# Squares for the norm bounds moved from VectorE to GpSimd in an attention and mixture-of-experts kernel

## The chip, the cores and the metric

The kernel runs on 8 cores of one Trainium2 chip. Each core takes one of the 8 batch entries (4096 tokens of width 1024) and runs the same program; the cores exchange nothing. The metric is the device time in microseconds (us) of the slowest core; lower is better.

## What is computed

The reference, cut to its core (16 heads of 64, 16 experts of inner width 512 of which the two best count, one shared expert of width 1024):

```python
def attn(x, Wq, Wk, Wv, Wo, bo):
    q, k, v = (x @ Wq), (x @ Wk), (x @ Wv)            # split into 16 heads
    w = softmax(q @ k.T / sqrt(64))
    return (w @ v) @ Wo + bo
def ffn(x, Wr, Wg, Wu, Wd, Sg, Su, Sd):
    shared = silu(x @ Sg) * (x @ Su) @ Sd
    cw = top-2 of softmax(x @ Wr), as a weight per token and expert
    routed = sum over e of (silu(x @ Wg[e]) * (x @ Wu[e]) @ Wd[e]) * cw[e]
    return routed + shared
x = layernorm(x + attn(x))
x = layernorm(x + ffn(x))
```

## The kernel before

The program is written as five instruction lists, one per engine, each run in order (`Prog.emit`; waits on semaphores are worked out from the `deps`). DMAs may be issued by SyncE, ScalarE and GpSimd. All DMAs of GpSimd that load weights or x count on one semaphore, and each waits for the one before it to have landed.

Stages: attention for the first 2048 queries (`attention_half(0)`), output projection and first layer norm for them (`wo_ln1_half(0)`), the same two for the other 2048 queries (`attention_half(1)`, `wo_ln1_half(1)`), and then the experts (`ffn_all`, from about 3480 us on).

An attention half runs over 8 pairs of heads `p` (128 channels), and in each over 4 query tiles `q` of 512. A tile has 32 steps `j` of 128 keys: two score matmuls (L528, L536), one exponential over 1024 columns on ScalarE (L551) and two matmuls with the values (L563, L571). The scores of step j+2 are issued in step j. The exponential has a bias that bounds the scores: minus the root of (largest squared norm of a query of the tile) times (largest squared norm of a key of the pair). These norms are what the change is about:

- Keys, `k_group` and `knorm_one`. `k_group(s, ki, kst)` makes 512 keys: 8 matmuls (L246), a VectorE copy from PSUM to `kt_v` (L253), a VectorE multiplication of these keys with themselves into `sqk[ki % 2]` (L260). `v_group` then makes 512 values with 32 short matmuls (L310) and two VectorE copies (L318, L325). `knorm_one` sums the squares over the channels with one TensorE matmul against ones (L272), VectorE takes the largest (L278) and merges it (L290). In the first half the keys and values of pair p+1 are made during the last query tile of pair p, one group ki after each fourth step (j = 3, 7, ... 31), and after pair 7 those of pair 0 once more for the second half. So there are 8 such windows with 8 groups each. Pair 0 of the first half gets its own from `kv_full` at the start. In the second half keys and values are read back instead (`kv_load_slice`: SyncE loads 8 slices of each, L344 and L350, after the same steps; each waits for the one before it to land).
- Queries, `q_chain_A` and `q_chain_B`. A: 8 matmuls (L412), a scaled VectorE copy into `qtb` (L420). B: a VectorE multiplication into `sqk[q % 2]` (L432), a TensorE sum (L444) and a VectorE maximum (L450). In the second half the chains of query tiles 0, 1, 2 of pair p+1 run in the last tile of pair p (A after steps 5, 9, 13, B one step later); that of tile 3 runs at the start of pair p+1. For pair 0 of the second half all four A and then all four B run at its start, and in the first half this holds for every pair.
- `q_chain_C_all` makes the bias from the four maxima (L464 to L487); the first exponential of a pair waits for it. `tail` divides the sums of the tile before by a VectorE reciprocal (L669, 6.5 us) and two multiplications (L674, L681); it is issued after step 2 of a tile.

What GpSimd's list holds during attention: only DMA issues. `load_qkv(p+1)` (L202) is emitted at the start of pair p and waits until the buffer's last user, `q_chain_A` of pair p-1, is done. After `attention_half(0)` comes the load of the output weights `wb[1][:, 0:8192]` (L1289), which has no `deps` beyond the weight DMA before it; the matmuls L720 of `wo_ln1_half(0)` read it. GpSimd's first multiplications (L1175) come in the expert stage.

## Time and profile before

| | |
|---|---|
| two timed runs | 6785.51 and 6828.65 us, median 6807.08 |
| the profiled execution | 6785.92 us |
| its span, slowest core (core 7) | 6784.4 us; the others from 6758.3 |
| mean granted TensorE clock of the cores | 0.942 to 0.945 |
| TensorE matmuls busy | 6045.8 us (89%) |
| VectorE busy | 2475.7 us (36%) |
| ScalarE busy | 2608.7 us (38%) |
| GpSimd busy | 729.6 us (11%), nearly all of it in the expert stage |

Busy times are sums over one profiled execution. Times in the trace are counted from the span's start. A row of the timeline gives the start, the duration, the engine (PE is TensorE, DVE VectorE, ACT ScalarE, POOL GpSimd; SPq is the queue of SyncE), the line and operation, and in brackets the idle time of that engine before it and what ended it.

### The profile page before, as it was taken

How to read it: one execution, taken by the hardware profiler on the slowest of the kernel's cores; microseconds unless marked ns; L12 is line 12 of the kernel's file. 1: busy time of each engine (PE TensorE's matmuls, PEld its weight loads, DVE VectorE, ACT ScalarE, POOL GpSimd, SP SyncE). 2: the span in 40 equal slices, each digit the busy share in tenths (PEclk: the TensorE clock that was granted, in tenths of full speed). 3: DMA queues.
4: the chain of work that ended last, by engine and by line, in shares of the span. 5: the costliest groups of instructions: out<-in, count | busy, mean ns of one | idle time of the engine just before them, and what ended most of it. 6: DMA issues, size and time to landing. Idle time of an engine off the chain costs nothing.

```text
span 6784.4 us, 78807 instructions; the slowest of 8 cores (6758.3 to 6784.4 us)
## 1 busy us (share of the span) xinstructions
PE 6045.8 (89%) x27000; PEld 2209.2 (33%) x27000; DVE 2475.7 (36%) x3406; ACT 2608.7 (38%) x2903; POOL 729.6 (11%) x683
## 2 busy tenths in 40 slices
PE   5898888888878888888889999999989999999995
PEld 2332233322322222222234444444433444444442
DVE  2333333333532222222433344434432443444345
ACT  2576655676257777777421111111122111111111
POOL 0000000000000000000001222222232222222220
PEclk8899989999889999989899999999999999999998
DMA  4000000000000000000112222222212222221111
GB/s 77 18 1 18 18 18 18 21 10 18 1 30 18 18 18 18 18 13 13 19 45 37 38 38 38 38 38 38 38 44 62 38 38 38 38 38 32 34 29 50
DMA packets 54615, 198.44 MB, mean 29 GB/s; under 512 B 5072, under 2 KB 27728, under 8 KB 37984
## 3 DMA queue, kind: packets, MB, share of 16 engines
q0 software_dynamic: 26496, 136.36, 11.3%
q1 hardware_dynamic: 25280, 44.46, 1.9%
q10 hardware_dynamic: 2464, 12.58, 0.5%
q8 instruction: 240, 3.93, 0.2%
q14 instruction: 135, 1.11, 0.1%
HBM read 291.85 MB, written 37.88 MB: 49 GB/s over the span
## 4 chain that ended last, share of the span: by engine, by line
PE 66%; ACT 17%; DVE 7%; issue 6%; DMA 4%; DVEq 0%; ACTq 0%; SPq 0%; POOLq 0%
ACT pt L551 16%; PE psA L1203 15%; PE psS L1150 15%; PE psS L1137 11%; PE psS L528 4%; PE psA L563 4%; PE psV L1137 4%; PE psA L571 3%; PE psS L720 2%; PE psV L310 2%; PE psM L246 1%; DVE recipb L669 1%; DMA wbB<-scr 1%; PE psM L658 1%; DMA xt<-xti 1%
## 5 line engine op out<-in xcount | busy, mean ns | idle before, releaser
L551 ACT ACTIVATE pt<-psS,biasb 128x1024 bf16<-128x1024 f32 x2048 | 2104.5, 1158 | 660.0 <-PE psS L536 622.4
L1158 ACT ACTIVATE sq<-psS 128x512 bf16<-128x512 f32 x432 | 257.9, 597 | 2251.1 <-PE psS L1137 2245.2
L528 PE MATMUL psS<-qtb,wbB 64*128 64x512 bf16 x2048 | 813.3, 402 | 199.0 <-ACT pt L551 86.4
L1164 DVE TENSOR_TENSOR abuf<-psS,sq 128x512 bf16<-128x512 f32 x576 | 398.4, 692 | 1615.8 <-PE psS L1150 1606.6
L563 PE MATMUL psA<-pt,wbA 128*65 128x512 bf16 x2048 | 874.3, 427 | 30.2 <-ACT pt L551 25.5
L536 PE MATMUL psS<-qtb,wbB 64*128 64x512 bf16 x2048 | 832.9, 412 | 0.0
L571 PE MATMUL psA<-pt,wbA 128*65 128x512 bf16 x2048 | 826.9, 404 | 0.0
L1175 POOL TENSOR_TENSOR abuf<-abuf,qtb 128x512 bf16<-128x512 bf16 x512 | 585.5, 1151 | 1558.4 <-DVE abuf L1164 1557.9
L1203 PE MATMUL psA<-abuf,wbB 128*128 128x512 bf16 x2304 | 560.4, 383 | 56.2 <-DVE xt L1231 21.4
L1203 PE MATMUL psA<-abuf,wbA 128*128 128x512 bf16 x2304 | 546.2, 379 | 21.7 <-ACT abuf L1223 4.7
L528 PEld LDWEIGHTS psS<-qtb,wbB 64*128 64x128 bf16 x2048 | 187.3, 94 | 1156.3 <-issue 1156.3
L1231 DVE TENSOR_TENSOR xt<-psA,xt 128x512 bf16<-128x512 f32 x544 | 376.3, 692 | 156.8 <-PE psA L1203 135.0
L1231 DVE TENSOR_TENSOR abuf<-psA,abuf 128x512 bf16<-128x512 f32 x544 | 376.3, 692 | 154.0 <-PE psA L1203 135.0
L626 DVE COPY astg<-psA 65x512 f32<-65x512 f32 x64 | 43.7, 682 | 1041.6 <-PE psA L571 1041.6
L669 DVE RECIPROCAL recipb<-recipb 64x1024 f32<-64x1024 f32 x64 | 418.9, 6545 | 6.6
L563 PEld LDWEIGHTS psA<-pt,wbA 128*65 128x65 bf16 x2048 | 225.7, 110 | 566.0 <-issue 566.0
L1203 PEld LDWEIGHTS psA<-abuf,wbB 128*128 128x128 bf16 x2304 | 197.2, 97 | 398.3 <-issue 230.8
L1203 PEld LDWEIGHTS psA<-abuf,wbA 128*128 128x128 bf16 x2304 | 195.1, 96 | 361.1 <-issue 190.7
L202 POOL DMA_DIRECT2D wbA<-attnw x14 | 7.4, 530 | 2677.1 <-PE psV L412 2677.1
L1150 PE MATMUL psS<-xt,wbB 128*128 128x512 bf16 x1152 | 273.5, 380 | 2.5 <-DVE abuf L1164 2.5
L1150 PE MATMUL psS<-xt,wbA 128*128 128x512 bf16 x1152 | 273.8, 381 | 0.0
L1150 PE MATMUL psS<-abuf,wbA 128*128 128x512 bf16 x1152 | 273.3, 380 | 0.0
(168 smaller groups left out, 5387.9 us busy)
## 6 DMA issues: line engine op xcount, KB each, us to landing
wbA<-moew POOLq DMA_DIRECT2D x54, 1024.0 KB, 7.9
wbB<-moew POOLq DMA_DIRECT2D x54, 1024.0 KB, 7.8
wbA<-attnw POOLq DMA_DIRECT2D x16, 768.0 KB, 7.0
scr<-wbA SPq DMA_DIRECT2D x8, 1040.0 KB, 4.1
xt<-xti POOLq DMA_DIRECT2D x8, 1024.0 KB, 8.9
scr<-wbB SPq DMA_DIRECT2D x8, 1024.0 KB, 3.9
out<-astg SPq DMA_DIRECT2D x16, 512.0 KB, 2.8
wbA<-scr SPq DMA_DIRECT2D x56, 130.0 KB, 2.1
```

The costliest lines, as they stand in the source:

```text
L528: e.matmul(psS[sl][:, 0:QT], kt_v[0:64, j * 128:(j + 1) * 128], qtb[0:64, sl_q * QT:(sl_q + 1) * QT], start=True, stop=True),
L536: e.matmul(psS[sl][:, QT:E2], kt_v[64:128, j * 128:(j + 1) * 128], qtb[64:128, sl_q * QT:(sl_q + 1) * QT], start=True, stop=True),
L551: e.activation(pt[:, sl * E2:(sl + 1) * E2], psS[j % 2][:, 0:E2], AF.Exp, bias=biasb[:, sl_q:sl_q + 1]),
L563: e.matmul(psA[0][0:65, :], va_v[:, j * 130:j * 130 + 65], pt[:, sl * E2:sl * E2 + QT], start=(j == 0), stop=(j == NJ - 1)),
L571: e.matmul(psA[1][0:65, :], va_v[:, j * 130 + 65:j * 130 + 130], pt[:, sl * E2 + QT:sl * E2 + E2], start=(j == 0), stop=(j == NJ - 1)),
L669: lambda e: e.reciprocal(recipb[:, 0:E2], recipb[:, 0:E2]),
L1137: e.matmul(gp[:, go:go + QT], wb[sl][:, kc * 512 + fc * 128: kc * 512 + (fc + 1) * 128], xsrcs[h](kc, q), start=(kc == 0), stop=(kc == NCH ...
L1150: e.matmul(up[:, uo:uo + QT], wb[sl][:, 4096 + kc * 512 + fc * 128: 4096 + kc * 512 + (fc + 1) * 128], xsrcs[h](kc, q), start=(kc == 0), s ...
L1164: e.tensor_tensor(abuf[:, hb + fc * QT:hb + (fc + 1) * QT], up[:, uo:uo + QT], sq[:, :], ALU.mult),
L1175: e.tensor_tensor(abuf[:, hb + fc * QT:hb + (fc + 1) * QT], abuf[:, hb + fc * QT:hb + (fc + 1) * QT], qtb[:, q * QT:(q + 1) * QT], ALU.mult),
L1203: e.matmul(pa[:, 0:QT], wb[sl][:, 8192 + fc * 1024 + mc * 128: 8192 + fc * 1024 + (mc + 1) * 128], abuf[:, hb + fc * QT:hb + (fc + 1) * QT ...
L1231: e.tensor_tensor(acc_ap(h, mc, q), pa[:, 0:QT], acc_ap(h, mc, q), ALU.add),
```

## The change

The multiplications of `k_group` in the windows of the first half (8 pairs times 8 groups, 64 in all) and those of `q_chain_B` in the second half (8 pairs times 4, 32 in all) go from VectorE to GpSimd. They signal GpSimd's semaphore instead of VectorE's. Those of `kv_full` and of `q_chain_B` in the first half stay on VectorE. The instructions stand in GpSimd's list where the calls emit them, between the DMA issues.

```diff
-            def k_group(s, ki, kst):
+            def k_group(s, ki, kst, eng2="vector"):
...
-                sqt = P.emit("vector",
+                sqt = P.emit(eng2,
                              lambda e, ki=ki:
                                  e.tensor_tensor(sqk[:, (ki % 2) * QT:(ki % 2 + 1) * QT],
                                                  kt_v[:, ki * QT:(ki + 1) * QT],
                                                  kt_v[:, ki * QT:(ki + 1) * QT],
                                                  ALU.mult),
-                             deps=[ev, war["sqk%d" % (ki % 2)]], inc="dve",
+                             deps=[ev, war["sqk%d" % (ki % 2)]],
+                             inc="pl" if eng2 == "gpsimd" else "dve",
                              nochain=True)
...
                 def q_chain_B(q, qe):
...
-                    qs = P.emit("vector",
+                    qs = P.emit("gpsimd" if h == 1 else "vector",
...
-                                deps=[qe, war["sqk%d" % (q % 2)]], inc="dve",
+                                deps=[qe, war["sqk%d" % (q % 2)]],
+                                inc="pl" if h == 1 else "dve",
                                 nochain=True)
...
                             if h == 0:
-                                k_group(ns[1], ki, nkst)
+                                k_group(ns[1], ki, nkst, eng2="gpsimd")
```

## Rows read from the trace of the kernel before

**Rows 1.** The page: shares of the chain that ended last, by engine.

```profile
PE 66%; ACT 17%; DVE 7%; issue 6%; DMA 4%; DVEq 0%; ACTq 0%; SPq 0%; POOLq 0%
```

**Rows 2.** Waits of TensorE: total us, times, longest; the first from L444's own view.

```profile
  DVE sqk L432: 92.1, 64
...
PE psM L272 <- DVE sqk L260: 34.4, 8, 5.6
PE psS L528 <- DMA wbB<-scr: 32.1, 7, 6.6
```

**Rows 3.** View of line 1175, a GpSimd multiplication: ns min/median/max, first and last start.

```profile
L1175 POOL TENSOR_TENSOR abuf<-abuf,qtb x512: 1138/1152/1169, 3628.1 to 6688.0; 128x512 bf16<-128x512 bf16 x171
```

**Rows 4.** Timeline, second group (ki = 1) of pair 0's window, first half.

```profile
259.27 0.69 DVE L253 CAST wbB<-psM 128x512 bf16<-128x512 f32 x1 [5.59 <-PE psM L246]
260.06 0.42 DVE L260 TENSOR_TENSOR sqk<-wbB 128x512 bf16<-128x512 bf16 x1
260.81 0.38 PE L272 MATMUL psM<-sqk,ones_c 128*1 128x512 bf16 x1
...
261.61 3.12 ACT L551 ACTIVATE pt<-psS,biasb 128x1024 bf16<-128x1024 f32 x3 [3.58 <-PE psS L536]
```

**Rows 5.** Timeline, first group (ki = 0) of the same window.

```profile
250.69 0.69 DVE L253 CAST wbB<-psM 128x512 bf16<-128x512 f32 x1
...
252.06 0.38 PE L272 MATMUL psM<-sqk,ones_c 128*1 128x512 bf16 x1 [3.94 <-DVE sqk L260]
```

**Rows 6.** Timeline, after the last group (ki = 7) of the same window.

```profile
307.27 1.89 PE L412 MATMUL psM<-xt,wbA 128*128 128x512 bf16 x8 [1.73 <-DVE rowsA L290]
```

**Rows 7.** Timeline in the expert stage: VectorE to GpSimd and back.

```profile
5020.50 0.69 DVE L863 CAST ab<-psM 128x512 bf16<-128x512 f32 x1 [0.17 <-DVE xt L1231]
5021.33 2.12 POOL L1052 TENSOR_TENSOR outst<-xt,ab 128x1024 f32<-128x1024 bf16 x1 [21.86 <-DVE ab L863]
...
5023.51 0.69 DVE L1118 CAST qtb<-psM 128x512 bf16<-128x512 f32 x1 [1.00 <-POOL outst L1052]
```

**Rows 8.** Output weights: GpSimd's issue, the last copy of keys, first reading matmuls.

```profile
1352.55 0.53 POOL L1289 DMA_DIRECT2D wbB<-woi  x1 [6.66 <-DMA wbA<-attnw]
...
1744.26 0.69 DVE L253 CAST wbB<-psM 128x512 bf16<-128x512 f32 x1 [3.45 <-PE psM L246]
...
1753.38 3.60 PE L720 MATMUL psS<-abuf,wbB 128*128 128x512 bf16 x8
```

**Rows 9.** DMA issues: KB each, us from issue to landing.

```profile
wbB<-woi POOLq DMA_DIRECT2D x1, 2048.0 KB, 14.9
```

**Rows 10.** Timeline, second half, pair 1's window, chain B of query tile 2.

```profile
2250.00 0.38 PE L444 MATMUL psM<-sqk,ones_c 128*1 128x512 bf16 x1 [0.60 <-DVE sqk L432]
```

**Rows 11.** Timeline, second half, start of pair 2, then of pair 6.

```profile
2268.65 0.69 DVE L420 TENSOR_SCALAR qtb<-psV 128x512 bf16<-128x512 f32 x1 [17.49 <-PE psV L412]
2269.15 0.53 POOL L202 DMA_DIRECT2D wbA<-attnw  x1 [173.35 <-PE psV L412]
...
2277.99 3.19 ACT L551 ACTIVATE pt<-psS,biasb 128x1024 bf16<-128x1024 f32 x3 [4.76 <-DVE biasb L487]
...
2968.02 0.69 DVE L420 TENSOR_SCALAR qtb<-psV 128x512 bf16<-128x512 f32 x1 [17.70 <-PE psV L412]
...
2973.65 3.19 ACT L551 ACTIVATE pt<-psS,biasb 128x1024 bf16<-128x1024 f32 x3 [1.05 <-DVE biasb L487]
```

**Rows 12.** Timeline of SyncE's queue, pair 1's window: keys 3, keys 7, values 7.

```profile
2251.39 0.32 SPq L344 DMA_DIRECT2D wbB<-scr  x1
...
2270.22 0.32 SPq L344 DMA_DIRECT2D wbB<-scr  x1
...
2276.35 0.32 SPq L350 DMA_DIRECT2D wbA<-scr  x1
```

**Rows 13.** Timeline, start of the second half: last chain A, last sum of B.

```profile
1916.18 0.69 DVE L420 TENSOR_SCALAR qtb<-psV 128x512 bf16<-128x512 f32 x1 [2.25 <-PE psV L412]
...
1922.68 0.58 PE L444 MATMUL psV<-sqk,ones_c 128*1 128x512 bf16 x1 [1.26 <-DVE sqk L432]
```

## The prediction, made before the changed kernel ran

> **What bounds the kernel now.** I read the page first. Its chain of work that ended last lies two thirds on TensorE and hardly on VectorE [rows 1], so freeing VectorE is worth little by itself. The question is what stands behind each square: a TensorE matmul that sums it, and TensorE runs its list in order. The waits say where that already hurts: the sums of the queries' squares (L444) waited 64 times, the sums of the keys' squares (L272) 8 times, and the scores (L528) 7 times for a slice of keys [rows 2]. Then the timeline around one case of each kind, and GpSimd's and SyncE's queues.
>
> In a window of the first half the second group shows the usual case. The copy of the keys starts at 259.27, VectorE squares them at 260.06 for 0.42 us, done at 260.48, and the sum starts at 260.81 without a wait, because TensorE was busy until then with the values [rows 4]. So the square was ready 0.33 us early, no more. Behind the sum stand the scores of the next step, and ScalarE had idled 3.58 us for them [rows 4]: here TensorE sets the end, and a wait of TensorE is lost one for one. In the first group VectorE is late, since the reciprocal is ahead of the copy; the sum waited 3.94 us and started 1.37 us after the start of the copy [rows 5]. This 1.37 us is the bare path copy, square, sum.
>
> **The price of a square on GpSimd.** The expert stage has the same operation on the same shape, 512 times, at 1138 to 1169 ns [rows 3]; I take 1.15 us. GpSimd started 0.14 us after the end of the VectorE instruction that it waited for (5020.50 + 0.69 to 5021.33), and VectorE 0.06 us after one of GpSimd's (5021.33 + 2.12 to 5023.51) [rows 7]. TensorE waiting for GpSimd is not in the trace. TensorE after VectorE takes 0.15 us, from rows 4 and 5 (1.37 less 0.69, less 0.10 to the square's start, less 0.43 us); I take 0.15, with 0.06 as the lower end and 0.3, twice the nearest row, as the upper. The path becomes 0.69 + 0.14 + 1.15 + 0.15 = 2.13 us instead of 1.37: **+0.76 us** where the path is bare.
>
> The Trainium skill, GPSIMD Engine Reference, section Engine selection, calls GpSimd about 2 times slower than VectorE for two-input elementwise work and says to keep it on VectorE; the rows make it 1.15 to 0.42, 2.7 times. With twice 0.42 each of the 77 exposed paths below would be 0.3 us shorter, and the whole sum about 32 instead of 55 us. The measurement decides; the advice itself holds here.
>
> **First half, 64 squares.** First groups (8 windows): bare path, 8 x 0.76 = 6.1 us. Groups 1 to 6 (48): the sum started 1.54 us after the start of the copy [rows 4], now 2.13: 48 x 0.59 = 28.3 us. Each of the pairs that I looked at has the same 1.54. Last groups: the next matmuls wait for the maximum (L278, L290), not for the sum [rows 6], and the maximum stands behind the copies of the values on VectorE; the sum is 0.6 us later, but most of that was waiting anyway; 0.1 us each, 7 x 0.1 = 0.7. What VectorE saves, 0.42 us per group, is worth nothing: its next instruction waits for the values. Sum: **+35.1 us**.
>
> **What is queued behind the squares.** GpSimd's list is in order too. `load_qkv(p+1)` now stands behind the 8 squares of pair p, so it is issued at the end of the window instead of a whole pair earlier. Its first users come with the window after, over 100 us on: free. The output weights are another matter. Their load was issued at 1352.55, long before use [rows 8]. Now it stands behind the last square of the last window: copy at 1744.26 + 0.69 + 0.14 + 1.15 = 1746.24. It takes 14.9 us [rows 9], so it lands at 1761.2. The first matmul that reads them started at 1753.38 [rows 8], and nothing else is on TensorE then; it starts at about 1761.3. The VectorE work in between (reciprocal and multiplications) is done by then, and the projection is bound by TensorE afterwards, so the wait is not made up: **+7.9 us**. Cover gone entirely would be 14.9; landing in half the time would leave 0.3.
>
> **Second half, 32 squares.** Three chains in each of 7 windows. They waited already (0.60 us for tile 2, [rows 10]; tile 0 longer, behind the reciprocal), so all are bare: 21 x 0.76 = **+16.0 us**. ScalarE has run dry there too, so nothing hides it.
>
> The chain of tile 3 is at the start of pairs 1 to 7. There two things race: the bias, and slice 7 of the keys. At pair 6 nothing disturbs the slice, and from the copy L420 to the first exponential it is 2973.65 - 2968.02 = 5.63 us; at pair 2 it is 2277.99 - 2268.65 = 9.34 us [rows 11]. The reason is L202, issued at 2269.15, 1.07 us before slice 7 of the keys at 2270.22; the slice landed only at 2276.35, 6.13 us later [rows 11, 12]. So the bias has 3.7 us to spare and +0.76 costs nothing at pairs 1 to 5, where L202 collides; at pair 7 it costs 0.76.
>
> But the change moves L202. It now stands behind the squares of tiles 0 to 2, so it goes out just after the third of them, in the window, about 1.5 us before slice 3. That looks like a gain of 3.7 us less 0.76 at five starts. I don't count it: from slice 3 to the landing of slice 7 the queue is a chain without gaps, 9 transfers in 2276.35 - 2251.39 = 24.96 us [rows 12], each issued when the last has landed. If slice 3 is the one that takes 6.1 us, slice 7 lands at the same time. L202 leads its slice by 0.4 us more than now: 5 x -0.4 = -2.0. Pair 6 gets a collision that it did not have; between 0.76 and 3.7 I take 1.2, as part of the delay meets slack ahead of slice 4. With pair 7: **about 0**.
>
> The Trainium skill, DMA: Bandwidth & Descriptors, the paragraph on Arbitration, says that a DMA engine takes turns between its queues, packet by packet. Then a slice of 2.1 us beside a load should take about 4.2 us, an estimate, and five starts would gain 1.9 us each, 9 us in all. The slice's 6.13 us says otherwise.
>
> Start of the second half: four B chains in a row. On VectorE each square had to wait for the maximum of the chain before, so from the last copy at 1916.18 to the last sum at 1922.68 went 6.50 us [rows 13]. GpSimd can do squares 0 and 1 while TensorE still runs chains A; 2 and 3 follow sums 0 and 1. Copy 3 ends at 1916.87; sum 0 runs before it ends, square 2 ends near 1917.8, square 3 near 1918.95, last sum near 1919.1: **-3.6 us**.
>
> **The sum.** 35.1 + 7.9 + 16.0 + 0 - 3.6 = **+55 us**. On the profiled execution's own 6785.9 us this gives 6841. The median of the two runs is 21 us above that, but one of them is at 6785.5, so I add only 4: **6845 us**, 0.8% above 6785.9.
>
> **Rivals.**
> - *The slices catch up.* If the moved L202 does not delay slice 7 (slack in the queue, or the sharing above), five starts lose up to 3.7 - 0.76 = 2.9 us each: -15 us; and with 0.06 us for GpSimd to TensorE another 77 x -0.09 = -7. Sum +33, 6819 us. Against it: the gapless queue [rows 12].
> - *The clock of TensorE falls after the longer waits.* Eight matmuls took 1.89 us after an idle of 1.73 us [rows 6], 0.22 us from one to the next, the level of 2.4 GHz; eight others took 3.60 us [rows 8], the level of 1.2 GHz. A fall costs such a group 1.7 us. The waits of tiles 1 and 2 grow from 0.60 to 1.36 us; if those 14 lower the clock, +24 us: 6865. This is also the case on the other side: if the 48 new waits of 0.59 us did it too, 62 x 1.7 = +105 us on top, 6946, 2.3% slower; it decides from 81 further us, 48 falls, on. Against both: the 1.73 us idle without a fall.
> - *The squares are hidden after all,* because the cover in rows 4 is wider than the modelled matmul ends show. Then the first half costs only 6.1 + 0.7, and the sum is +27 us, 6813. With the slices catching up too it would be about +12; below 6786 only with the output weights on time as well.
>
> **Chances.** Forecast as summed 0.60 (its own range 6820 to 6870, from 0.06 to 0.3 us per hand-over and the load of the output weights between 0.3 and 14.9 us); slices catch up 0.12; squares hidden 0.08; clock falls in the second half 0.15; clock falls everywhere 0.03; no slower than before 0.02. The range of 8 in 10 is 6808 to 6890. Two per cent (136 us), about what a measurement of this kernel can tell from no change, is reached by the clock everywhere alone: faster 0.01, within 0.96, slower 0.03.
>
> **What would show it.** In the profile after: L272 waits for GpSimd's `sqk` in 64 cases instead of 8, about 0.6 us in most; L444 waits in the second half 0.76 us longer, 1.36 for tiles 1 and 2; GpSimd's squares last 1.15 us; L1289 is issued near 1781 us (1746 plus the 35 gained by then), and L720 waits for it; L202 of the second half stands between the third square and slice 3, and slice 3 takes 6 us to land; the first exponential of pairs 1 to 5 is still about 9 us behind its L420. The expert stage keeps its length. I am wrong if the squares last other than 1.15 us, if matmuls of 0.4 us and more follow the new waits, if the waits of TensorE do not lengthen the gaps of ScalarE, or if slice 7 lands early.

## The result, and the profile after

| | before | after |
|---|---|---|
| profiled execution, slowest core's span | 6784.4 us | 6839.5 us |
| profiled execution, time | 6785.9 us | 6841.08 us |
| median core's span | 6773.8 us | 6829.0 us |

The ratio of the two kernels is **1.0076, 95% interval 1.006 to 1.0092**: 0.8% slower, which is less than the two per cent taken as the line. Most executions of both kernels, run side by side, fell into a slower state of the chip in which the cores of one die or both show a lower granted clock (medians of all: 7241.5 us after, 7251.6 before), so every number below is taken from executions, or cores, outside it. The median core is the median of the spans of all cores, over all executions of a kernel, whose granted clock was 0.94 or more. The change of the profiled execution is 6839.5 - 6784.4 = +55.1 us in span, and 0.76% of 6790 us is +52. The sum of the prediction was +55, to 6841 us.

The page after (slowest core: core 1), the row of engines and the chain that ended last; the chain answers to [rows 1]:

```profile
PE 6064.0 (89%) x27000; PEld 2212.3 (32%) x27000; DVE 2435.5 (36%) x3310; ACT 2610.3 (38%) x2903; POOL 829.1 (12%) x779
...
PE 65%; ACT 17%; DVE 7%; issue 6%; DMA 4%; POOL 1%; DVEq 0%; ACTq 0%; POOLq 0%; SPq 0%
```

GpSimd has come into the chain with 1%, and that is the whole matter: it is busy for 12% of the span, far from any bound as an engine, and it still costs. The waits of TensorE (total us, times, longest) say where; they answer to [rows 2]:

```profile
PE psM L273 <- POOL sqk L260: 68.7, 64, 6.3
PE psM L446 <- POOL sqk L433: 42.5, 14, 5.8
...
PE psV L446 <- POOL sqk L433: 25.0, 15, 2.2
PE psM L446 <- DVE sqk L433: 20.3, 16, 1.3
...
PE psS L530 <- DMA wbB<-scr: 19.3, 6, 3.4
...
PE psS L722 <- DMA wbB<-woi: 7.5, 1, 7.5
```

The sums of the keys' squares (now L273) wait in all 64 groups of the windows where 8 waited before. The scores' wait for a slice of keys (now L530) went from 32.1 us on the slowest core before to 19.3 on the slowest core after; and there is a new wait of 7.5 us for the output weights. The second group of pair 0's window, the timeline that answers to [rows 4]:

```profile
259.14 0.69 DVE L253 CAST wbB<-psM 128x512 bf16<-128x512 f32 x1 [6.77 <-PE psM L246]
...
260.04 1.04 POOL L260 TENSOR_TENSOR sqk<-wbB 128x512 bf16<-128x512 bf16 x1 [9.42 <-PE psV L311]
...
261.22 0.38 PE L273 MATMUL psM<-sqk,ones_c 128*1 128x512 bf16 x1 [0.47 <-POOL sqk L260]
...
262.02 2.12 ACT L553 ACTIVATE pt<-psS,biasb 128x1024 bf16<-128x1024 f32 x2 [4.32 <-PE psS L538]
```

From the copy's start to the sum it is now 261.22 - 259.14 = 2.08 us (before 1.54), and ScalarE's gap grew from 3.58 to 4.32 us. From one copy of keys to the next such a group took 7.45 us and takes 7.99: +0.54, the whole of the longer path, in group after group.

To place the time, the core was cut into stretches by landmarks of the timeline (means over the 8 cores of the profiled execution, us). This is arithmetic on the timeline's start times, no view:

```
stretch                                        before   after   difference
start to first exponential                      122.5   122.7    +0.2
first half, windows of pairs 0 to 6            1433.5  1458.2   +24.7
last pair, to first matmul of projection        191.8   203.5   +11.7
projection to last chain A                      162.6   162.7     0.0
start of 2nd half: last copy to first exp.       20.3    17.1    -3.2
second half, windows                           1154.4  1171.4   +17.0
second half, starts of pairs 1 to 7 (sum)        48.9    53.8    +4.9
after the last pair, to the experts             301.3   301.2     0.0
experts                                        3338.6  3338.9    +0.3
```

TensorE's granted clock stands at one of two levels, 1.2 or 2.4 GHz, and its share at the lower one can be read for each stretch. On the mean core TensorE was at the lower level for 237.1 us in the windows of the first half before and 231.1 after, and in the windows of the second half for 177.5 before and 187.4 after. These figures are needed below, where a stretch differs from its sum.

### The profile page after: what moved, and what is told of

Its sections match the earlier page's. It is cut to its first block, busy times and chain, and to the rows that moved or that the text cites. A ratio compares the mean times of both kernels' runs of the same rounds, so it can differ in the third digit from the quotient of the medians.

```text
span 6839.5 us, 78989 instructions; the slowest of 8 cores (6820.7 to 6839.5 us)
## 1 busy us (share of the span) xinstructions
PE 6064.0 (89%) x27000; PEld 2212.3 (32%) x27000; DVE 2435.5 (36%) x3310; ACT 2610.3 (38%) x2903; POOL 829.1 (12%) x779
## 4 chain that ended last, share of the span: by engine, by line
PE 65%; ACT 17%; DVE 7%; issue 6%; DMA 4%; POOL 1%; DVEq 0%; ACTq 0%; POOLq 0%; SPq 0%
ACT pt L553 16%; PE psA L1205 15%; PE psS L1152 15%; PE psS L1139 11%; PE psS L530 4%; PE psA L565 4%; PE psV L1139 4%; PE psA L573 3%; PE psS L722 2%; PE psM L246 1%; DVE recipb L671 1%; DMA wbB<-scr 1%; PE psM L660 1%; DMA xt<-xti 1%; PE psM L650 1%
## 5 line engine op out<-in xcount | busy, mean ns | idle before, releaser
L530 PE MATMUL psS<-qtb,wbB 64*128 64x512 bf16 x2048 | 816.2, 404 | 186.3 <-ACT pt L553 85.9
L530 PEld LDWEIGHTS psS<-qtb,wbB 64*128 64x128 bf16 x2048 | 187.2, 94 | 1149.9 <-issue 1149.9
L1152 PE MATMUL psS<-abuf,wbB 128*128 128x512 bf16 x1152 | 273.0, 380 | 0.0
```

The lines of the kernel that those rows point to most:

```text
L530: e.matmul(psS[sl][:, 0:QT], kt_v[0:64, j * 128:(j + 1) * 128], qtb[0:64, sl_q * QT:(sl_q + 1) * QT], start=True, stop=True),
L1152: e.matmul(up[:, uo:uo + QT], wb[sl][:, 4096 + kc * 512 + fc * 128: 4096 + kc * 512 + (fc + 1) * 128], xsrcs[h](kc, q), start=(kc == 0), s ...
```

## The experiments

Each kernel ran on all 8 cores beside the kernel before. By the median core the kernel before has 6773.8 us (6772.0 to 6777.3 from batch to batch), and the changed kernel 6829.0.

**e1: the first half alone.** The queries' squares back on VectorE.

```
-                    qs = P.emit("gpsimd" if h == 1 else "vector",
+                    qs = P.emit("vector",
```

> Only the 64 squares of the first half are on GpSimd; the second half is as before. My theory (each bare path grows by what the square and its hand-over last, TensorE's waits are lost one for one, and the output weights come late): with the sizes read in the changed kernel, 8 x 0.71 + 48 x 0.54 = 31.6 us, and 7.5 us for the output weights, 39 us over the kernel before in all; L202 of the second half goes out early as before, so the pair starts of the second half keep their times. Rival (the squares are hidden and something in the second half costs the time): under 10 us over the kernel before.

Measured: ratio 1.0048 (0.9992 to 1.0103); median core 6814.3 us, +40.5. The waits of TensorE for e1:

```profile
PE psM L273 <- POOL sqk L260: 66.8, 64, 6.3
...
PE psS L530 <- DMA wbB<-scr: 30.8, 6, 6.3
```

The interval of the ratio takes in 1, so the total alone doesn't settle it; the stretches do. Windows and last pair measured +24.2 and +12.4 us, 36.6 together where 39 were expected, as in the full change. The seven starts of pairs in the second half sum to 48.2 us on the mean of the cores (48.9 before), so whatever moved them in the full change lies in the other edit.

**e2: the second half alone.** The keys' squares back on VectorE.

```
-                                k_group(ns[1], ki, nkst, eng2="gpsimd")
+                                k_group(ns[1], ki, nkst)
```

> Only the 32 squares of the second half are on GpSimd; the first half and the load of the output weights are as before. My theory: 21 x 0.71 = 15 us in the windows, -3.2 us at the start of the half (four chains in a row), about 0 to 3 at the pair starts: 12 to 15 us over the kernel before. Together with the first run it should add up to the changed kernel's 50 to 54 us. Rival (the longer waits lower the granted clock of TensorE in the windows): 35 us or more, with matmuls of 0.4 us and more behind the waits of 1.3 us.

Measured: 6805.7 us in one execution; median core 6796.8, +23.0, more than expected. On the four cores of the profiled execution with a clock of 0.94 (0 to 3), the first half is as before (1435.9 and 191.2), the start of the second half is 17.1 (-3.2), its windows 1171.3 (+16.9), and the seven starts of pairs 54.2 us instead of 48.9 (+5.3). The windows and the start came as summed; the starts of pairs did not. 23.0 and e1's 40.5 add to 63.5 where the whole change has +55.2 by the same median. Of the 8 us too many, e1's part can be placed: its windows of the second half measured +5.4 and the stretch behind the last pair +2.3, though its edit doesn't touch them. In these windows TensorE was at the lower clock for 190.6 us where the kernel before has 177.5. So this is the scatter between executions, and a reason to read terms from stretches and not from totals. The rival (35 us or more, from the clock) is not borne out.

**e3: the output weights early.** The changed kernel with the load of the output weights emitted at the start of pair 7, ahead of pair 7's squares on GpSimd.

```
                     load_qkv(0)
+                    wo_box.append(P.emit(
+                        "gpsimd",
+                        lambda e: e.dma_start(wb[1][:, 0:8192], woi),
+                        inc="qw"))
...
-            tk_wo = P.emit("gpsimd",
-                           lambda e: e.dma_start(wb[1][:, 0:8192], woi),
-                           inc="qw")
+            tk_wo = wo_box[0]
```

> The changed kernel with one move: the load of the output weights is emitted at the start of pair 7 of the first half, ahead of that window's squares in GpSimd's list. My theory: the wait of 7.5 us of TensorE for the weights goes, the projection is bound by TensorE behind it, so the kernel is 7.5 us shorter than the changed one (1.0065 of the kernel before). Rival (the wait only stands where VectorE's reciprocal would be awaited anyway): 0 to 3 us shorter.

Measured: median core 6823.1, -5.9 against the changed kernel; last pair to projection 196.3 instead of 203.5, **-7.2**; the wait for the weights is gone from the list. This is what the position of one DMA issue behind a square cost. The timeline of the changed kernel shows it directly:

```profile
1773.19 0.59 POOL L1291 DMA_DIRECT2D wbB<-woi  x1
...
1787.95 3.57 PE L722 MATMUL psS<-abuf,wbB 128*128 128x512 bf16 x8 [7.52 <-DMA wbB<-woi]
```

Issued at 1773.19 after the last square, read at 1787.95: 14.8 us from the issue to the first matmul, of which TensorE waited 7.52. Before, the issue had a lead of 400 us [rows 8].

**e4: where the load of the next weights stands.** The kernel before, squares on VectorE, but with L202 held back until the third query square of the window, as GpSimd's order does it in the changed kernel.

```
-                    if not (h == 0 and p == 0):
+                    if not (h == 0 and p == 0) and not (h == 1 and p >= 1):
                         load_qkv(p + 1)
...
+                                    if qi == 2 and p + 2 < NP:
+                                        load_qkv(p + 2, [qs_box[0]])
```

> The kernel before, all squares on VectorE, with one move: in the second half the load L202 of pair p+2 goes out behind the third query square of the window of pair p, where the change put it. My theory: the load's collision moves from slice 7 of the keys to slice 3, slice 7 lands at nearly the same time because the slices queue without gaps. From the last copy of a query tile to the first exponential of the next pair: pairs 1 to 5 within 0.5 us of the kernel before, pair 6 up to 2 us longer; in all within 3 us of the kernel before. Rival (the slices catch up): 5.6 us at pairs 1 to 5, 10 to 15 us shorter in all.

Measured: median core 6784.7, +10.9, but the slowest core 6791.2 beside 6784.4. Rows of e4, first the scores' wait for a slice of keys, then two of the cores' spans:

```profile
PE psS L531 <- DMA wbB<-scr: 35.1, 6, 6.7
```

```profile
core 2: 6780.7 us, clock 0.941
...
core 4: 6791.2 us, clock 0.939
```

The moved load costs, and gains nothing: pairs 1 to 6 now start 8.5 to 9.0 us after their copy on the mean of the cores (single starts 7.4 to 10.6), and the sum over seven starts is 58.3 us on the mean. On cores that had started in about 9.4 us at pairs 1 to 5 this is the small gain that was expected there, but pair 6 grew from 5.63 to 8.8, more than the 2 us allowed for, and the +10.9 in all are outside the 3 us expected. 58.3 against a mean of 48.9 before shows why: on some cores of the kernel before these starts had been cheaper. The eight cores one by one:

```
sum of the 7 starts, us   core 0    1      2      3      4      5      6      7
before                    57.91  39.50  39.48  57.98  58.53  39.48  39.49  58.96
after                     58.96  49.84  58.22  49.40  53.05  53.97  57.88  48.96
```

39.5 is 7 x 5.63, a start at which the keys are in time. In the kernel before this holds for all seven starts on four cores; on the other four, pairs 1 to 5 start 9.1 to 10.0 us after the copy. The spans of the kernel before, per core, follow that:

```profile
core 1: 6765.9 us, clock 0.944
core 2: 6758.3 us, clock 0.945
core 3: 6782.2 us, clock 0.944
core 4: 6783.1 us, clock 0.942
```

And this is the start of pair 2 on core 1 of the kernel before, the place of [rows 11, 12] on another core:

```profile
2262.98 0.32 SPq L344 DMA_DIRECT2D wbB<-scr  x1
...
2263.18 0.69 DVE L420 TENSOR_SCALAR qtb<-psV 128x512 bf16<-128x512 f32 x1 [17.52 <-PE psV L412]
...
2263.67 0.53 POOL L202 DMA_DIRECT2D wbA<-attnw  x1 [173.77 <-PE psV L412]
...
2265.13 0.32 SPq L350 DMA_DIRECT2D wbA<-scr  x1
...
2268.81 3.19 ACT L551 ACTIVATE pt<-psS,biasb 128x1024 bf16<-128x1024 f32 x3 [1.05 <-DVE biasb L487]
```

Here slice 7 of the keys is issued 0.69 us *ahead* of L202 and lands in 2.15 us (values 7 is issued at 2265.13). On core 7 it was issued 1.07 us *behind* L202 and landed after 6.13 us [rows 11, 12]. Less than two microseconds in the order of two transfers decide over 5.63 or about 9.3 us. The load collides on core 1 too, only one slice later, with the last slice of values (L350). The view of L350 on core 1:

```profile
DMA to landing us min/median/max: 2.0/2.1/6.2
```

At pairs 1 to 5 the last slice of values takes 5.5 to 6.2 us there (4.3 at one start on core 5), but its first reader (L563, behind the first exponential) comes later than the first scores: it starts 1.9 us after the first exponential where nothing is late, and 1.9 to 2.6 us after it at these starts of cores 1 and 2. So all eight cores have the collision, and it costs 3.7 us or so only where it meets the last slice of keys. What makes the order differ: on cores 0, 3, 4 and 7 one or two earlier transfers of slices take together 1.2 to 2.1 us longer in each of these windows. Why they do, the traces do not show. It isn't a property of the core: in the profiled execution of e11 (below), whose second half has the same windows, it is cores 1, 3, 4 and 6 that sum to 39.5.

**e7: the load out of the way.** The kernel before, with L202 for pair p+2 held until the end of query tile 0 of pair p, in the middle of the pair where no slice is under way.

```
-                    if not (h == 0 and p == 0):
+                    if not (h == 0 and p == 0) and not (h == 1 and p >= 1):
...
+                    if h == 1 and q == 0 and p + 2 < NP:
+                        load_qkv(p + 2, [s_tok[NJ - 1]])
```

> The kernel before with one move: in the second half the load L202 of pair p+2 waits for the end of the first query tile of pair p, where no slices of keys are under way. My theory (slice 7 of the keys lands late on those cores where L202 is ahead of it): from the last copy of a query tile to the first exponential of the next pair it is 5.6 us on all cores and at all pair starts; cores 0, 3, 4 and 7 are 15 to 19 us shorter, the other four stay, and the slowest core is 12 to 18 us shorter than before. Rival (the slice is late for another reason than L202): no change.

Measured: ratio 0.9971 (0.9929 to 1.0013); median core 6767.6. Every pair on every core starts in 5.6 to 5.7 us, sum 39.5. The slowest core of the profiled execution has 6775.6 us, 8.8 less than the kernel before and not 12 to 18, and the ratio does not set the kernel apart from it: the expectation holds for the stretch and is not shown for the total. The view of the keys' slices (L344) on core 7, before and then e7, and e7's wait of the scores there:

```profile
DMA to landing us min/median/max: 2.0/2.1/6.6
```

```profile
DMA to landing us min/median/max: 2.0/2.0/2.3
...
PE psS L528 <- DMA wbB<-scr: 1.4, 2, 1.1
```

On this core no slice of keys takes longer than 2.3 us without a load beside it (2.5 on any core), and the wait for them falls from 32.1 us [rows 2] to 1.4. So the 6 us landings, and the wait, come from the overlap with L202. The Trainium skill, DMA: Bandwidth & Descriptors, the paragraph on Arbitration, lets queues take turns, packet by packet; with even turns a slice of 2.1 us beside a load should take about 4.2 us, an estimate. The runs show 5.9 to 6.6 us for the slices read here, so the slice loses more than an even share. Whether packets of different size do it was not tested.

**e9: twice the delay.** The changed kernel with each of the 64 key squares done twice on GpSimd.

```
+                if eng2 == "gpsimd":
+                    sqt = P.emit(eng2,
+                                 lambda e, ki=ki:
+                                     e.tensor_tensor(sqk[:, (ki % 2) * QT:(ki % 2 + 1) * QT],
+                                                     kt_v[:, ki * QT:(ki + 1) * QT],
+                                                     kt_v[:, ki * QT:(ki + 1) * QT],
+                                                     ALU.mult),
+                                 deps=[sqt], inc="pl", nochain=True)
```

> The changed kernel with each of the 64 key squares of the first half done twice on GpSimd, one after the other; the sum waits for the second. My theory: each wait of TensorE grows by a square and a hand-over within GpSimd, about 1.04 + 0.15 = 1.2 us, and every such wait is lost one for one, except for the last group of a window, which loses some 0.8 us: 8 x 1.2 + 48 x 1.2 + 8 x 0.8 = 74 us over the changed kernel, all of it between the first and the last pair of the first half. The output weights go out 1.2 us later, so L722 waits 0.4 us longer or shorter. Rival (part of the wait is made up by ScalarE's slack in the steps between groups): 40 us or less.

Measured: ratio 1.0182 (1.0063 to 1.0301); cores at about 6936 us (none has a clock of 0.94), +107 against the changed kernel. Waits, timeline of pair 1's window, two stretches of it from sum to sum and clock on core 2 of e9 (the second square is L270):

```profile
PE psM L281 <- POOL sqk L270: 145.8, 64, 7.5
```

```profile
494.75 0.38 PE L281 MATMUL psM<-sqk,ones_c 128*1 128x512 bf16 x1 [1.65 <-POOL sqk L270]
...
495.93 0.39 PE L538 MATMUL psS<-qtb,wbB 64*128 64x512 bf16 x1
...
503.92 0.38 PE L281 MATMUL psM<-sqk,ones_c 128*1 128x512 bf16 x1 [1.65 <-POOL sqk L270]
...
507.74 0.60 PE L538 MATMUL psS<-qtb,wbB 64*128 64x512 bf16 x1
```

```profile
core 2: us, PE busy (x) PEld busy (x) DVE busy (x) ACT busy (x) POOL busy (x), PEclk, DMA share, GB/s
494.75:503.92 9.17, 7.41 (x57) 3.71 (x58) 2.27 (x5) 4.13 (x4) 2.08 (x2) 1.00 0.01 2
503.92:514.45 10.53, 8.83 (x57) 3.85 (x58) 2.28 (x5) 4.35 (x4) 2.08 (x2) 0.84 0.00 0
```

```profile
core 2: 6941.6 us, clock 0.937
```

Two things are seen. The group's period is 9.17 us in most groups, 7.99 + 1.18: the second square lengthens the path by 1.18 us, and all of it is paid, so the squares stand wholly on the path. And some groups are longer: of the 48 per core between the second and the last copy of a window, 13 to 19 take about 10.5 instead of 9.17 us. The two stretches above are neighbours, each behind the same wait of 1.65 us. In the first the granted clock (PEclk) was 1.00; in the second it was 0.84, and a matmul took 0.60 instead of 0.39 us. On all eight cores each of the long groups has such a fall of the clock and none of the others has. About 16 times 1.3 is 21 us of the 33 us beyond the expected 74. With the waits of 0.47 us of the changed kernel the same 48 groups have no fall on any core and nearly all take 7.99 (the last of each window 7.64). So the rival of the clock names something that does happen, but in the first half not at the size of wait that this change makes.

**e5: the kernel before, with the sums later.** If the sum is what waits, it may be issued later: `knorm_one` after step 6, 9, 13, ... instead of 3, 7, 11, ..., and the B chains at 8, 12, 16 instead of 6, 10, 14.

```
-                                and p + 1 < npair and j in (5, 6, 9, 10, 13, 14)):
+                                and p + 1 < npair and j in (5, 8, 9, 12, 13, 16)):
...
+                        if ns is not None and h == 0 \
+                                and j in (6, 9, 13, 17, 21, 25, 29):
+                            knorm_one(nkst)
```

> The kernel before, all squares on VectorE and all loads where they were; only the TensorE sums of the squares stand later in its list: those of the keys after step 6 for the first group and two steps behind each other group, those of the queries in the second half after steps 8, 12 and 16 instead of 6, 10 and 14. My theory (a wait of TensorE in these windows is lost one for one): the waits of 3.9 us for the first key group (8) and of 3.7 and 0.6 us for the query chains (7 and 14) shrink by two to three steps of about 1 us each, and TensorE's clock has less reason to fall after them: 8 x 3 + 7 x 2.2 + 14 x 0.6 = 48 us shorter than the kernel before. Rival (ScalarE or the slices of keys set the time there anyway): under 10 us shorter.

Measured: median core 6709.0, **-63**, more than the 48 expected: first half 1405.2 (-28.3), windows of the second 1125.5 (-28.9), last pair -3.9. The waits of the keys' sums on the profiled core (34.4 us before, [rows 2]):

```profile
PE psM L272 <- DVE sqk L260: 12.6, 8, 3.0
```

In the windows of the second half the sums of tiles 1 and 2 no longer wait at all, and that of tile 0 mostly waits 1.8 instead of 3.7 us. That the gain is above the sum lies in part in the clock: TensorE was at the lower level for 213.1 us in the windows of the first half (237.1 before) and for 167.9 in those of the second (177.5).

**e6: the changed kernel, with the same two edits and the weights early.** If the cost of GpSimd is only delay, it has to vanish where a later sum covers it.

```
+                                and p + 1 < npair and j in (5, 8, 9, 12, 13, 16)):
...
+                                and j in (6, 9, 13, 17, 21, 25, 29):
+                            knorm_one(nkst)
...
+            tk_wo = wo_box[0]
```

> The changed kernel (squares on GpSimd) with the same later sums as the run before, and the output weights loaded early. My theory: the square's 1.04 us and its hand-over are now covered by two steps of attention in groups 1 to 7 and in tiles 1 and 2, so of the 50 us of the change only 0.7 us at each of 15 first groups and tiles and about 1 us at the pair starts remain, less 3 at the start of the second half: within 15 us of the run with the sums later and VectorE's squares. Rival (GpSimd's squares cost by themselves, by contention or the clock, not by TensorE's wait): 35 us or more over it.

Measured on the four cores of the profiled execution with a clock of 0.94 or more (0 to 3): 6718.4 to 6730.9, their upper three within 0.4 us; median core **6730.9**, so +22 over e5 where the changed kernel is +55 over the kernel before. That is above the 15 us expected and below the 35 of the rival. First half: 1407.0 against e5's 1405.2, so of 24.7 us only 1.8 are left. Windows of the second half: +12.4 of 17.0 are left; of the rest, the starts of pairs have +3.5 and the start of the half -3.2. The waits of e6:

```profile
PE psM L274 <- POOL sqk L261: 24.1, 16, 3.7
```

The keys' squares are hidden once two or three steps lie between them and their sum. So are the queries' squares of tiles 1 and 2: on these cores their sums wait 0.00 us in every window, in e5 as in e6. That of tile 0 mostly waits 2.5 us where e5 has 1.8, seven times 0.7 = 5 us, as expected. The other 7 us go with the clock: in these windows TensorE was at the lower level for 184.7 us in e6 and 167.9 in e5. Whether GpSimd's squares cause that or it is scatter (e1's untouched windows varied by as much), these runs do not separate.

**e8: both repairs of the kernel before** (e5's and e7's edits together).

```
+                                and p + 1 < npair and j in (5, 8, 9, 12, 13, 16)):
...
+                                and j in (6, 9, 13, 17, 21, 25, 29):
+                            knorm_one(nkst)
...
+                    if h == 1 and q == 0 and p + 2 < NP:
+                        load_qkv(p + 2, [s_tok[NJ - 1]])
```

> The kernel before with both moves, the sums later and L202 in the middle of a pair, squares on VectorE. My theory: both gains add up, 48 + 15 = about 60 us shorter than the kernel before (0.991), the fastest of all. Rival (with TensorE's waits gone the slices of keys, which queue without gaps, set the end of the windows): half of it or less, with new waits of L528 for slices at the pair starts.

Measured: ratio 0.9883 (0.982 to 0.9945); median core 6708.8, 63 us below the kernel before where about 60 were expected, and executions from 6722.4 us. The starts of pairs sum to 39.7 us where e5 has 51.6, with all other stretches of the attention as in e5. The median core of all executions doesn't show these 12 us (6709.0 in e5); that of the four cores of the profiled execution shows 9 of them (6713.8 in e5, 6704.6 in e8). So e7's saving is seen in its stretch and is unclear in the total.

**e11: the squares on GpSimd where four stand in a row.** The kernel before, with only the batches at the start of a pair moved (36 squares), none of the windows'.

```
-                def q_chain_B(q, qe):
+                def q_chain_B(q, qe, pool=False):
...
-                    qs = P.emit("vector",
+                    qs = P.emit("gpsimd" if pool else "vector",
...
-                       else q_chain_B(qq, _qe[qq]) for qq in range(nq)]
+                       else q_chain_B(qq, _qe[qq], not pre)
+                       for qq in range(nq)]
```

> The kernel before with only those query squares on GpSimd that come four in a row at the start of a pair (all 8 pairs of the first half and pair 0 of the second, 36 squares). My theory: GpSimd does the first two while TensorE still runs the chains A, and the other two no longer queue behind the maxima on VectorE; 3.2 us shorter each, as at the start of the second half of the changed kernel: 9 x 3.2 = 29 us shorter than the kernel before. Rival (the first half hides these chains behind the write-back or the bias in another way): 3 us only, from the one start that the changed kernel shows.

Measured: median core 6751.8, **-22** (-25 against the kernel before in its own batch). From the last copy to the first exponential 10.77 became 7.20 us at the pairs of the first half, and 20.3 became 15.45 at the start of the second. Eight times 3.57 and 4.85 would be 33 us; part of it is given back elsewhere, for instance in the windows of the second half, whose code is the same and which took 1162.0 instead of 1154.4 us, with TensorE at the lower clock for 194.6 us instead of 177.5. The timeline of such a batch in e11:

```profile
517.57 0.69 DVE L420 TENSOR_SCALAR qtb<-psV 128x512 bf16<-128x512 f32 x1 [1.03 <-PE psV L412]
517.91 2.16 POOL L432 TENSOR_TENSOR sqk<-qtb 128x512 bf16<-128x512 bf16 x2 [1.86 <-PE psM L445]
...
520.22 0.38 PE L445 MATMUL psV<-sqk,ones_c 128*1 128x512 bf16 x1 [0.48 <-POOL sqk L432]
```

The square is 2.5 times as long as on VectorE and the batch is still shorter: on VectorE each square stood in the list behind the maximum of the chain before it, and on GpSimd it does not.

**e10: e8 and e11 together.**

```
+                       else q_chain_B(qq, _qe[qq], not pre)
...
+                                and j in (6, 9, 13, 17, 21, 25, 29):
+                            knorm_one(nkst)
...
+                        load_qkv(p + 2, [s_tok[NJ - 1]])
```

> The kernel before with three moves: the sums later, L202 in the middle of a pair, and the squares on GpSimd only where four chains come in a row. My theory: the gains add up, 0.9883 for the first two and 29 us for the third: about 0.984 of the kernel before, 6680 us. Rival (some gains overlap, for instance GpSimd's squares delay the loads behind them): 0.988, no better than the first two moves.

Measured: ratio **0.9821 (0.9735 to 0.9907)**; executions from 6688.3 us, median core 6687.0. Page of e10:

```profile
span 6708.2 us, 78900 instructions; the slowest of 8 cores (6673.7 to 6708.2 us)
...
PE 67%; ACT 18%; DVE 6%; issue 6%; DMA 2%; DVEq 0%; POOL 0%; ACTq 0%; POOLq 0%; SPq 0%
```

It is faster than both kernels, about 87 us ahead of the kernel before by the median core, as summed (0.984 expected). VectorE's share of the chain fell from 7% to 6% and DMA's from 4% to 2%.

## Why the prediction was right, and where it was not

**What bounds, and the sign.** Right. TensorE waits at its own sum and ScalarE's idle time grows with it; e1 and e9 show it one for one. That freeing VectorE is worth nothing is right too: the square left VectorE in 96 places, and the one place that got shorter is the start of the second half.

**The price of a square.** Mis-sized twice, in opposite directions. The square took 1.04 us and not 1.15 (L260 has 1028/1038/1040 ns): the rows of the expert stage [rows 3] multiply two different tiles and write into one of them, and here both inputs are the same tile and the output is another. The start after VectorE took 0.20 to 0.21 us and not 0.14 (260.04 less 259.14 + 0.69). TensorE after GpSimd took 0.14, predicted 0.15. The bare path is 2.08 us: +0.71 instead of +0.76, and +0.54 instead of +0.59 in groups 1 to 6. The Trainium skill, GPSIMD Engine Reference, section Engine selection, has GpSimd about 2 times slower; 1.04 to 0.42 is 2.5 times, so this trace stands nearer the row than the rule, and its advice to keep such work on VectorE holds for the windows and fails for the batches (e11).

**First half, +35.1.** The seven windows of pairs 0 to 6 were summed at 7 x 0.76 + 42 x 0.59, about 30, and measured +24.7; the last pair's window and the weights at 4.3 + 7.9, and measured +11.7. Of the 5 to 6 us too many in the windows, 49 x 0.05 = 2.5 are the price of the path. The other 3 us lie outside the groups: from the first to the last copy of keys the seven windows grew by 27.8 us (373.1 to 400.9), which is 7 x 0.71 + 42 x 0.54 = 27.7, and the time outside shrank by 3.0 us, with TensorE at the lower clock there for 196.7 us instead of 205.6. So the mechanism and its corrected price are met within 0.2 us where they act.

**Output weights, +7.9.** Right, measured 7.5 as a wait and 7.2 by removal (e3).

**Windows of the second half, +16.0.** Measured +17.0, which is nearer than the parts deserve. With the bare path of +0.71 it would be 21 x 0.71 = 14.9, and where the clock was alike on both sides it is: core 0 took 1149.8 us before and 1163.9 after, +14.1, with 169.0 and 168.3 us at the lower level. On the mean core that time grew from 177.5 to 187.4 us, which is about the rest.

**Start of the second half, -3.6.** Measured -3.2. The way there was partly other: the last copy to the last sum shrank more, from 6.50 us [rows 13] to 1953.26 - 1950.61 = 2.65 in these rows of the changed kernel, but what follows gave 0.65 of it back.

```profile
1950.61 0.69 DVE L421 TENSOR_SCALAR qtb<-psV 128x512 bf16<-128x512 f32 x1 [2.24 <-PE psV L413]
1950.96 2.16 POOL L433 TENSOR_TENSOR sqk<-qtb 128x512 bf16<-128x512 bf16 x2 [4.97 <-PE psM L446]
...
1953.26 0.59 PE L446 MATMUL psV<-sqk,ones_c 128*1 128x512 bf16 x1 [0.48 <-POOL sqk L433]
```

**Starts of pairs, about 0.** This is the mis-sized term from which there is most to learn. The mechanism was read rightly: L202 does stand between the third square and slice 3, and slice 3 takes the delay. Core 1 of the changed kernel, pair 1's window:

```profile
2289.12 0.59 POOL L202 DMA_DIRECT2D wbA<-attnw  x1
...
2290.70 0.32 SPq L345 DMA_DIRECT2D wbB<-scr  x1
2296.64 0.32 SPq L351 DMA_DIRECT2D wbA<-scr  x1
...
2311.50 0.32 SPq L345 DMA_DIRECT2D wbB<-scr  x1
2313.64 0.32 SPq L351 DMA_DIRECT2D wbA<-scr  x1
2315.28 3.19 ACT L553 ACTIVATE pt<-psS,biasb 128x1024 bf16<-128x1024 f32 x3 [1.98 <-DVE biasb L489]
```

Slice 3 takes 2296.64 - 2290.70 = 5.94 us, and from its issue to the landing of slice 7 it is 22.94 us instead of 24.96 [rows 12]; the 24.96 held one more slow transfer, of 3.4 us. Two things made the size wrong. The term rested on one core: the slowest, from which rows 11 and 12 come, was one of four on which the load met the last slice of keys; on the other four it cost nothing, and for them the moved load is a new cost. And where the load had met that slice, the starts did not stay at about 9 us on each core: pairs 1 to 5 take 6.8 to 7.4 us on core 7 and 8.4 to 9.5 on core 0, so the rival of the slices that catch up (chance 0.12) came true in part on some cores. Core 7 went from 58.96 to 48.96, **-10 us**; cores 1, 2, 5 and 6 went from 39.5 to between 49.8 and 58.2, **+10 to +19**; the mean is +4.9. In spans, the four cores whose keys were in time before went from 6764.3 to 6828.4 us on the mean, +64, the other four from 6783.4 to 6830.5, +47. The slowest core after (core 1) is one of the first kind and the slowest before (core 7) one of the second: +55.1 is a difference between two different cores, and that it meets the sum of 55 is partly chance.

**The clock.** The rival was given 0.15 for the waits of tiles 1 and 2 of 1.36 us. Here are one such wait and the group behind it in the changed kernel:

```profile
2282.29 0.38 PE L446 MATMUL psV<-sqk,ones_c 128*1 128x512 bf16 x1 [1.32 <-POOL sqk L433]
...
2285.24 1.89 PE L413 MATMUL psM<-xt,wbA 128*128 128x512 bf16 x8
```

Eight matmuls in 1.89 us, the level of 2.4 GHz: no fall behind 1.32 us. Of the 112 such waits in the seven windows on eight cores, the granted clock fell behind one (core 4, the window of pair 4). The time at the lower level did grow in these windows, by 9.9 us (177.5 to 187.4), but in e1, whose second half is that of the kernel before, it is 190.6; so these runs do not tie it to the squares. In e9, a wait of 1.65 us in each group brought a fall in about a third of the groups. The argument against the rival leaned on one idle of 1.73 us without a fall [rows 6], a single wait; a wait that comes back in each group is another matter, so the reasoning was thinner than its result.

**The last step, from the sum to a time.** This is the step that failed. "On the profiled execution's own 6785.9 us this gives 6841", and there the changed kernel is at 6841.08. But then the prediction took the two executions that it had seen, 6785.5 and 6828.7 us, as the level of all, added 4 us, and gave 6808 to 6890 for the time of any. What the runs showed instead: the median of all executions is 7241.5 us for the changed kernel and 7251.6 for the kernel before, some 6% above the levels of 6845 and 6786 that the prediction used for them. No row stood behind that step: each term in it was a difference, the range was worked out from the bounds of those differences, and two executions say next to nothing of how a kernel's time is spread. The forecast should have been stated as a difference, +55 us within +22 to +104 (6808 and 6890 less 6786), to be added to whatever level the kernel before shows beside it.

## What to carry to other kernels

Price an operation that moves to another engine by the bare path between its neighbours (two hand-overs and its own length), and then look at what covers that path: here a path longer by 0.54 us, paid in every group, was most of the first half's cost, and a sum issued two or three steps later took nearly all of it away. Move along with it everything that stands behind it in the new engine's queue, DMA issues first: one load of weights issued 420 us later cost 7.5 us. The slower engine is worth it where it breaks a chain of dependence in a list (four squares behind four maxima), not where it lengthens one; and before a term rests on a race of two transfers, read it on all cores, not on the slowest.

## What of the hardware was not expected

- GpSimd squares a 128x512 bf16 tile in 1.04 us, and multiplies two different ones in 1.14 to 1.17 [rows 3]. Which part of the difference (a second input tile, an output that is one of the inputs) makes the 0.1 us was not tested.
- The hand-overs with GpSimd: VectorE to GpSimd 0.20 us, GpSimd to TensorE 0.14 us.
- A slice of keys that mostly lands in 2.0 to 2.5 us (single ones up to 3.8 in e8) takes 5.6 to 6.7 us in the kernel before when issued behind a load of weights, and 2.1 us when issued 0.69 us ahead of it; then it is the slice of values behind it that takes 5.5 to 6.2 us. The same program shows both outcomes on different cores, at the same five starts: sums of 39.5 or about 58 us. Which cores are which differs between the profiled executions of the kernel before, e1, e5 and e11.
- With a wait of 1.65 us in each group of 9.17 us (e9), 13 to 19 of 48 groups per core took about 1.3 us longer, each with a fall of the granted clock (0.84 over one such group). With 0.47 us in each there was no fall, and with 1.32 us twice in a window of the second half one in 112. Sizes between these were not tried.
- Open: why one or two transfers of slices take together 1.2 to 2.1 us longer in each of five windows, on cores 0, 3, 4 and 7 of the kernel before; and what makes the time at the lower clock vary by some 15 us between windows of the same code.
